# Phase 0 of a macaron layer (mixture of experts, linear attention, mixture of experts): fewer filler matmuls ahead of the first up, the first downs between the first ups, and single tiles normalised and transposed behind the ups

## The chip, the cores and the metric

One core of one Trainium2 chip runs the whole program. The metric is device time in microseconds, the median of several executions. The engines are PE (TensorE), DVE (VectorE), ACT (ScalarE), POOL (GpSimd) and SP (SyncE, which here only issues DMAs). They run in parallel, each through its own list of instructions in order, and wait for each other on semaphores.

## What is computed

x is 2 x 2048 x 128, float32. Every expert of the feed-forward blocks maps 128 to 512 and back to 128.

```python
x = x + 0.5 * ffn(layernorm(x))      # 4 experts, each row goes to the argmax of its gate
x = x + attn(layernorm(x))           # linear attention, features elu(.) + 1 of 32 projections
x = x + 0.5 * ffn(layernorm(x))      # the same weights again

def ffn(x):
    idx = argmax(softmax(x @ Wg + bg))
    h = gelu(x @ W1[e] + b1[e])      # for each expert e
    y = h @ W2[e] + b2[e]
    return y of expert idx
def attn(x):
    q, k, v = x @ Wq.T, x @ Wk.T, x @ Wv.T
    q_, k_ = elu(q @ proj) + 1, elu(k @ proj) + 1
    return q_ @ (k_.T @ v) / sum(q_)     # per batch
```

## The kernel before

The two batches pass through the two feed-forward blocks one after the other, so there are four phases, ph = 0 to 3: block 0 of batch 0, block 0 of batch 1, block 1 of batch 0, block 1 of batch 1. The attention of a batch lies beside the phases that follow.

**Tiles and visits.** The 2048 rows of a batch are sorted by expert. DVE and PE work out for each place of the sorted order which row stands there (route_hot, route_slots, route_hots, inverse, route_src), POOL gathers the rows by indirect DMA, one DMA per tile of 128 rows (L433, T = 16 tiles), and the phase computes V = 19 visits, a visit being a tile with one expert; where a tile holds rows of two experts it is visited twice, and a mask chooses the rows. s = ph * 19 + v numbers the visits.

**One visit** goes through these helpers:
- norm (DVE, L699) subtracts the mean of a gathered tile and multiplies by its deviation's inverse, into one of 8 buffers xn. It waits for the gather.
- turn_in (PE, L954) transposes one or two such tiles (a "group", by the table GROUPS) into the one PSUM bank TR, and copy_in (ACT, L1138) copies them to hT_in.
- copy_slab (SP, L342) copies the visit's first weights, with bias, to one of 7 buffers slab; the first few copies also wait for a norm, slab(s) for the norm of tile s-1 (L351).
- up (PE, L963) multiplies, 4 matmuls written as 8 instructions, into one of 3 PSUM banks U; it waits for copy_in of its tile (need, L959), for its slab and for the gelu three visits back.
- gelu (ACT, L1144) is 4 instructions from U to one of 5 buffers hT.
- down (PE, L974) multiplies by W2 into one of 2 banks DN; it waits for its gelu and for the finish two visits back.
- residual (L711) adds the second bias to the rows, finish (L723) the result of down; both on DVE.

**The order is written out by hand.** Every engine has its own loop over s. On PE, step s of the loop does down(s), then the groups due at this step (GROUP_AT, L210, by groups_of), then up(s+3) (UP_LEAD = 3). On ACT it does the copy_in of the due groups, then gelu(s+3). On DVE it does finish(s), then the norms due (NORM_LATE for phase 0, L213, by norms_of), then residual(s+2), then statistics and routing. In phase 0 tiles 0 to 3 are turned in before the loop, tile 4 at step 0, tile 5 at step 1, and after that two tiles at a time at steps 2, 4, 6, 8 and 10; the norms of tiles 5 to 15 stand at steps 0, 1, 1, 2, 3, 4, 5, 6, 6, 8 and 9. In step s POOL waits for finish(s-1) (begun, L449) and issues the gather of tile s+8; between two gathers it clears a scratch tile (rested, L419), and in steps 3 and 4 a power (pow_front, L399) takes the place of that.

**Beside phase 0** lie the routing of batch 1 (hot_at = HOT0 = 5: route_hot on DVE at the end of step 5, L615 to L623; counts on PE in step 7, L927; route_slots on DVE at the end of step 6, L628 to L640, which waits for counts; route_hots in step 7, L645; inverse on PE in step 9, L937; route_src on DVE in step 9; the visit tables at the end of step 10, L652 to L676) and the attention's side work of batch 0 (side_turn on PE at L988 and side_kq at L995, the TURNS at v = 9, 12 and 15 and one in the next phase; la_scaled on DVE at L744, steps 10, 13 and 16). la_sum (PE, L1006) belongs to the first steps of phase 1.

**Ahead of phase 0**, busy(n) (L895) issues n filler matmuls of 128 x 128 float32, two instructions each, whose results nobody reads. 24 calls stand before tile 0 is turned in, and 3 between turn_in and up of each of tiles 0, 1 and 2. DVE does norm(0) to norm(4), with the statistics and variance of batch 1 (front_stats, front_variance, L544 to L555) between them.

Of the kernel before, what the change touches and what calls it, by code (L numbers as in the profile page):

```python
# [34 lines left out]
def build(nc, x, wq, wk, wv, proj, w1, b1, w2, b2, wg, bg, out):  # L35
# [5 lines left out]
    NE, _, F = w1.shape  # L41
    R = proj.shape[1]
    NC = F // P
    T = L // P
# [22 lines left out]
    with ExitStack() as ctx:  # L67
# [141 lines left out]
        GROUPS = ((0, 1), (1, 1), (2, 1), (3, 1), (4, 1), (5, 1), (6, 2), (8, 2), (10, 2), (12, 2), (14, 2))  # L209
        GROUP_AT = (-4, -3, -2, -1, 0, 1, 2, 4, 6, 8, 10)  # L210


        NORM_LATE = (-5, -4, -3, -2, -1, 0, 1, 1, 2, 3, 4, 5, 6, 6, 8, 9)  # L213
        NORM_MID = (-6, -5, -4, -3, -2, -1, 0, 0, 2, 2, 3, 3, 5, 5, 6, 6)
# [1 line left out]

        def groups_of(ph, v):

            return ([(ph, j) for j, at in enumerate(GROUP_AT) if at == v] +
                    [(ph + 1, j) for j, at in enumerate(GROUP_AT) if at + V == v and ph + 1 < 2 * B])  # L220

        def group(ph, j):
            return ph * len(GROUPS) + j

        def group_of_tile(k):
            ph, t = divmod(k, T)
            return group(ph, max(j for j, (first, _) in enumerate(GROUPS) if first <= t))

        def norms_of(ph, v):
            def at(p):  # L230
                return (NORM_LATE, NORM_MID, NORM_EARLY, NORM_LATE)[p]
            return ([(ph, t) for t in range(T) if at(ph)[t] == v and (ph, v) != (0, 0)] +
                    [(ph + 1, t) for t in range(T) if ph + 1 < 2 * B and at(ph + 1)[t] + V == v])

        def tau(ph, t):
# [128 lines left out]
        def _(eng):  # L364
# [113 lines left out]
            for v in range(V):  # L478
                s = v
                begun(s)  # L480
                if v in (3, 4):
                    pow_front(1, v - 3)
                if v + EARLY0 < T:
                    gather(0, 0, v + EARLY0, second=v in (3, 4))
                if v == HOT0 + 2:
                    place_tiles(1)
                if v >= FIRST0:
                    gather(0, 1, v - FIRST0)
                attention_pow(0, v)
            for v in range(V):  # L490
                s = V + v
# [11 lines left out]
            for v in range(V):  # L503
                s = 2 * V + v
# [18 lines left out]
        def _(eng):  # L523
# [293 lines left out]
            front_stats(1, H, H + GS)  # L817
            norm(0, 1)
            front_stats(1, H + GS, T)
            norm(0, 2)  # L820
            front_variance(1, 1)
            norm(0, 3)
            load_rows(0, 0)
            for s in range(RES_LEAD):
# [2 lines left out]
            for s in range(2 * B * V):  # L827
                ph, v = divmod(s, V)
                f, b = divmod(ph, 2)
                o = ph - 1  # L830
                if ph in (1, 2) and v == 3:
                    la_kv(o)
                finish(s)
                if ph in (1, 2):
                    if v == 1:
                        la_features(o, 2, NG)
                        la_z(o, 0, NG)
                    if v == 2:
                        la_gt(o)
                    if v == 4:  # L840
                        lb_x2(o, 1)
                        lb_x2(o, 2)
                    if v == 5:
                        lb_x2(o, 3)
                r = (0, 1) if ph == 0 else (1, ph - 1)
                hot_at = HOT0 if ph == 0 else HOT1
                if ph in (1, 2) and v == hot_at + 2:
                    route_hots(ph + 1)
                if ph < B + 1 and v == hot_at + (3 if ph == 2 else 4):
                    route_src(*r)  # L850
                if ph == 0 and v == 0:
                    norm(0, 5)
                for ahead in norms_of(ph, v):
                    norm(*ahead)
                if ph in (1, 2) and v == 0:
                    la_scaled(o, NG - 1)
                if ph == 0 and v == hot_at + 2:
                    route_hots(1)
                if s + RES_LEAD < 2 * B * V and not full(s + RES_LEAD):
                    residual(s + RES_LEAD)  # L860
                if (ahead := chunk_ahead(s, RES_LEAD + 1)):
                    load_rows(*ahead)
                if ph == 0 and 11 <= v < 17:
                    split_b2(v - 11)
                if f == 0:
                    for t in stats_of(ph, v):
                        la_stat(b, t)
                    for g in range(NG - 1):
                        if v == VAR_AT[ph][g]:
                            la_variance(b, g)  # L870
                        if v == SCALED_AT[ph][g]:
                            la_scaled(b, g)
                if f == 0 and v == 18:
                    la_variance(b, NG - 1)
                if ph in (1, 2):
                    if v == 0:
                        la_features(o, 0, 2)
                    if v == 3:
                        lb_x2(o, 0)
                if ph < B + 1:  # L880
                    if v == hot_at:
                        route_hot(*r)
                    if v == hot_at + 1:
                        route_slots(*r)
                    if v == hot_at + 5:
                        visit_ends()
                        visit_tables(*r)
                        visit_masks(*r)
# [3 lines left out]
        def _(eng):  # L892
# [53 lines left out]
                expert_at.update({ph * V + v + i: e for i, e in enumerate(loaded(eng, v_exp, ph, v, D))})  # L946

            def turn_in(ph, j):
                first, n = GROUPS[j]
                need(eng, ffn["norm"], tau(ph, first + n - 1))  # L950
                need(eng, ffn["xTs"], group(ph, j) - 1)
                for i in range(n):
# [107 lines left out]
            front_gate(NG + 3)  # L1060
            load_visits(0, 0)
            eng.wait_ge(s_foldd, 6)
            busy(24)
            for t in range(UP_LEAD):
                turn_in(0, t)
                busy(3)
                up(t)
            turn_in(0, 3)
            eng.wait_ge(s_w["w2"], 16 * NE)
            for s in range(2 * B * V):  # L1070
                ph, v = divmod(s, V)
                hot_at = HOT0 if ph == 0 else HOT1
                o = ph - 1
                if ph in (1, 2) and v == 0:
                    side_turn(o, NG - 1)
                down(s)
                if ph in (1, 2):
                    if v == 3:
                        la_kv(o)
# [2 lines left out]
                        lb_num(o, 1)  # L1082
                    if v == 5:
                        lb_num(o, 3)
                for ahead in groups_of(ph, v):
                    turn_in(*ahead)
                if ph in (1, 2):
                    if v == 0:
                        side_kq(o, NG - 1)
# [5 lines left out]
                    inverse(ph + 1, 0, NG)  # L1095
                if s + UP_LEAD < 2 * B * V:
                    up(s + UP_LEAD)
                if (ahead := chunk_ahead(s, UP_LEAD + 1)):
                    load_visits(*ahead)
                if ph < B and v in TURNS:  # L1100
# [13 lines left out]
        def _(eng):  # L1114
# [18 lines left out]
                eng.activation(XR[0][:, lo:hi, 0:D], X0[0][:, lo:hi, :], ACT.Copy).then_inc(s_copied, 1)  # L1133

            def copy_in(ph, j):
                first, n = GROUPS[j]
                need(eng, ffn["xT"], group(ph, j))
                ffn["xTs"].done(eng.activation(hT_in[ph % 2][:, first * P:(first + n) * P], TR[:, 0:n * P], ACT.Copy))  # L1138

# [57 lines left out]
            copy_in(0, 0)  # L1197
            copy_in(0, 1)
            gelu(0)
            copy_in(0, 2)  # L1200
            gelu(1)
            copy_in(0, 3)
            gelu(2)
            for s in range(2 * B * V):
                ph, v = divmod(s, V)
                if ph in (1, 2) and v == 0:
                    side_copy((ph - 1) * NG + NG - 1)
                for ahead in groups_of(ph, v):
                    copy_in(*ahead)
                late = ph in (1, 2) and v in (0, 1, 2)  # L1210
                if ph in (1, 2):
                    o = ph - 1
# [8 lines left out]
                        la_q(o)  # L1221
                if s + UP_LEAD < 2 * B * V and not (late and v < 2):
                    gelu(s + UP_LEAD)
                if ph < B and v in TURNS:
                    side_copy(ph * NG + TURNS.index(v))
                hot_at = HOT0 if ph == 0 else HOT1
# [32 lines left out]
```

## Time and profile before

| | us |
|---|---|
| median of 3 executions | 232.36 |
| lowest and highest | 231.41, 233.33 |
| the profiled execution | 232.38 |
| its span, first to last instruction | 230.6 |

The span is what the rows below count in, from 0; 1.8 us lie around it. A row of a timeline gives the start in us, the duration in us, then engine, line, operation, what is written and read, the shape, and how many instructions of this kind follow each other (x8); in brackets how long the engine sat idle before it and what ended that. Consecutive instructions overlap, so the duration of one can reach past the start of the next. Busy over the span: PE 205.0 us (89%), DVE 158.2 (69%), POOL 158.9 (69%), ACT 129.0 (56%). The granted TensorE clock is 0.977 in the mean; it is full except near the end of the kernel.

### The profile page before, as it was taken

The numbers are of one execution on the slowest core, as the hardware profiler recorded it, in microseconds if no ns is written. First come the engines' busy times: TensorE is split into PE (matmuls) and PEld (weight loads), VectorE is DVE, ScalarE is ACT, GpSimd is POOL, SyncE is SP. The second block draws the span as 40 slices with busy tenths as digits, with TensorE's granted clock in tenths as the row PEclk, the third lists the DMA queues.
The fourth block names the chain that finished last, engine by engine and source line by source line (L and its number), as shares of the span: only waits on it lengthen the run. The fifth ranks groups of instructions, "written<-read, shape, count | busy, mean of one in ns | idle before, by whom it ended". The sixth has DMA issues, their size and how long they took to land.

```text
span 230.6 us, 6363 instructions
## 1 busy us (share of the span) xinstructions
PE 205.0 (89%) x1786; PEld 192.7 (84%) x1786; DVE 158.2 (69%) x633; ACT 129.0 (56%) x410; POOL 158.9 (69%) x222
## 2 busy tenths in 40 slices
PE   7889999985999989998999899999999999999700
PEld 7879999974899987778999797879899999999700
DVE  2799845459888979899978777899967454544300
ACT  0655057655746578436756568724776666766300
POOL 7223888971738786293274978869788888888775
PEclk9999999999999999999999999999999999999955
DMA  4998378782435553357405653435926867561111
GB/s 100 320 372 284 105 250 297 263 296 73 174 115 181 171 182 97 130 187 284 165 13 199 216 192 98 140 111 196 340 90 228 278 214 236 220 218 48 46 57 46
DMA packets 22502, 41.69 MB, mean 181 GB/s; under 512 B 3635, under 2 KB 8643, under 8 KB 22470
## 3 DMA queue, kind: packets, MB, share of 16 engines
q1 hardware_dynamic: 18496, 34.24, 40.5%
q0 software_dynamic: 3072, 6.82, 11.3%
q8 instruction: 16, 0.26, 0.4%
q10 hardware_dynamic: 902, 0.23, 0.4%
q14 instruction: 16, 0.13, 0.2%
HBM read 9.41 MB, written 6.82 MB: 70 GB/s over the span
## 4 chain that ended last, share of the span: by engine, by line
PE 27%; POOL 17%; DVE 13%; issue 11%; DMA 7%; DVEq 1%; POOLq 0%
PE U L963 11%; PE DN L974 11%; DMA G<-rows,src 7%; POOL out_dram L445 6%; POOL rest L419 4%; POOL G L433 3%; POOL RS L404 2%; DVE ST L790 2%; DVE SL L645 2%; POOL G L409 2%; DVE G L723 1%; DVE G L787 1%; PE TR L954 1%; PE S L1006 1%; PE S L1030 1%
## 5 line engine op out<-in xcount | busy, mean ns | idle before, releaser
L1144 ACT ACTIVATE hT<-U,slab 128x128 f32<-128x128 f32 x304 | 86.4, 370 | 50.1 <-PE U L963 49.2
L974 PE MATMUL DN<-W,hT 128*128 (+1 forms) x608 | 81.5, 277 | 1.7 <-DVE G L723 1.4
L963 PE MATMUL U<-hT_in,slab 128*128 (+1 forms) x608 | 81.8, 278 | 0.3
L974 PEld LDWEIGHTS DN<-W,hT 128*128 128x128 f32 x608 | 73.8, 192 | 2.8 <-issue 2.7
L963 PEld LDWEIGHTS U<-hT_in,slab 128*128 128x128 f32 x608 | 73.9, 192 | 1.8 <-issue 1.1
L433 POOL DMA_INDIRECT G<-rows,src x64 | 62.6, 978 | 13.9 <-issue 9.9
L723 DVE SCALAR_TENSOR_TENSOR G<-DN,mask,G 128x128 f32 (+1 forms) x76 | 26.4, 347 | 28.9 <-PE DN L974 25.8
L419 POOL MEMSET rest<- 128x512 f32 (+1 forms) x75 | 34.3, 457 | 8.5 <-DVE G L723 3.4
L445 POOL DMA_INDIRECT out_dram<-G x32 | 31.5, 983 | 9.0 <-issue 6.5
L699 DVE TENSOR_SCALAR xn<-G 128x128 f32<-128x128 f32 x64 | 22.3, 377 | 7.0 <-DMA G<-rows,src 6.9
L1138 ACT ACTIVATE hT_in<-TR 128x128 f32<-128x128 f32 (+1 forms) x44 | 14.5, 330 | 19.2 <-PE TR L954 18.8
L711 DVE SCALAR_TENSOR_TENSOR G<-slab,mask,G 128x128 f32 (+1 forms) x60 | 21.0, 350 | 6.0 <-DVE G L723 4.5
L404 POOL TENSOR_TENSOR RS<-VE,neghalf 128x4 f32<-128x4 f32 x8 | 8.3, 1040 | 12.6 <-DVE VE L735 12.5
L895 PE MATMUL DN<-mean_w 128*128 128x128 f32 x104 | 14.4, 297 | 1.3 <-POOL mean_w L365 1.1
L954 PE MATMUL TR<-ident,xn 128*128 128x128 f32 x64 | 14.4, 277 | 0.8 <-DVE xn L699 0.8
L895 PEld LDWEIGHTS DN<-mean_w 128*128 128x128 f32 x104 | 13.6, 210 | 1.4 <-POOL mean_w L365 1.1
L465 POOL TENSOR_TENSOR AV<-A,lane_f 128x256 bf16<-128x256 bf16 x4 | 3.3, 834 | 14.9 <-DVE A L640 14.9
L409 POOL TENSOR_TENSOR G<-VE,neghalf 128x4 f32<-128x4 f32 x8 | 8.3, 1054 | 5.0 <-DVE VE L793 4.9
L399 POOL TENSOR_TENSOR XR<-VE,neghalf 128x8 f32<-128x8 f32 x4 | 6.7, 1676 | 5.1 <-DVE VE L555 5.1
L728 DVE BATCH_NORM_STATS2 ST<-G 128x6 f32<-128x128 f32 x32 | 8.7, 286 | 1.8 <-issue 1.5
L954 PEld LDWEIGHTS TR<-ident,xn 128*128 128x128 f32 x64 | 8.4, 145 | 1.2 <-DVE xn L699 1.2
L645 DVE TENSOR_TENSOR SL<-slot_i,lane_b 128x512 bf16<-128x512 int32 x12 | 9.2, 816 | 0.0
(163 smaller groups left out, 220.2 us busy)
## 6 DMA issues: line engine op xcount, KB each, us to landing
slab<-W SPq DMA_DIRECT2D x76, 322.0 KB, 3.1
rows<-XR SPq DMA_DIRECT2D x4, 576.0 KB, 4.8
rows<-G SPq DMA_DIRECT2D x8, 288.0 KB, 2.1
X<-in_L_attn_x_dram SPq DMA_DIRECT2D x4, 256.0 KB, 6.5
XR<-in_L_attn_x_dram SPq DMA_DIRECT2D x2, 512.0 KB, 9.3
W<-in_L_ffn_W_dram SPq DMA_DIRECT2D x1, 1024.0 KB, 11.9
W<-in_L_ffn_W_dram SPq DMA_DIRECT2D x4, 256.0 KB, 5.8
G<-rows,src POOLq DMA_INDIRECT x64, 3.1
```

Of the source, the lines that this page charges most:

```text
L419: eng.memset(rest[:, 0:columns], 0.0)
L433: eng.indirect_dma_start(out=row(f, b, t, 0, RW), out_offset=None, in_=(rows0, rows1)[f][b], in_offset=bass.IndirectOffsetOnAxis(ap=src[f] ...
L445: eng.indirect_dma_start(out=out_rows, out_offset=bass.IndirectOffsetOnAxis(ap=index, axis=0), in_=row(1, b, t), in_offset=None, engine_se ...
L699: ffn["norm"].done(eng.tensor_scalar(xn[k % NXN][:, :], row(f, b, t), row(f, b, t, D, 1), row(f, b, t, D + 1, 1), ALU.subtract, ALU.mult))
L711: ffn["res"].done(eng.scalar_tensor_tensor(out=r, in0=slab[s % NSLAB][:, F + NC:SW], scalar=mask[f][b][:, v:v + 1], in1=r, op0=ALU.mult, o ...
L723: ffn["out"].done(eng.scalar_tensor_tensor(out=r, in0=DN[s % 2][:, 0:D], scalar=mask[f][b][:, v:v + 1], in1=r, op0=ALU.mult, op1=ALU.add))
L895: eng.matmul(DN[0][:, 0:P], mean_w[:, :], mean_w[:, :], start=True, stop=True)
L954: last = eng.transpose(TR[:, i * P:(i + 1) * P], xn[k % NXN][:, :], ident[:, :])
L963: i = eng.matmul(U[s % 3][:, c * P:(c + 1) * P], slab[s % NSLAB][:, c * P:(c + 1) * P], hT_in[ph % 2][:, bass.ds(v * P - expert_at[s], P)] ...
L974: i = eng.matmul(DN[s % 2][:, 0:D], hT[s % NHT][:, c * P:(c + 1) * P], W2[:, bass.ds(expert_at[s] + c * NE * D, D)], start=(c == 0 and not ...
L1138: ffn["xTs"].done(eng.activation(hT_in[ph % 2][:, first * P:(first + n) * P], TR[:, 0:n * P], ACT.Copy))
L1144: i = eng.activation(hT[s % NHT][:, c * P:(c + 1) * P], U[s % 3][:, c * P:(c + 1) * P], ACT.Gelu, bias=slab[s % NSLAB][:, F + c:F + c + 1])
```

## The change

The tables: phase 0 gets groups of one tile each (GROUPS0), tile t at step t - 4 (GROUP_AT0), and its norms stand at the same steps (NORM_SINGLE), so the norm of tile t for t of 5 to 15 is in step t - 4. In steps 0 to 11 of phase 0 (late_turns) PE turns a tile in after up(s+3) instead of before it, and ACT copies it after gelu(s+3) instead of before it. Ahead of the loop PE does busy(10) instead of busy(24) and no fillers ahead of up(2); down(0) is done after up(1), down(1) after tile 3 is turned in; the loop's downs run one visit ahead in steps 1 to 3 (downs_of) and as before from step 5. POOL's two powers and the gathers that go with them without a clearing move from steps 3 and 4 to steps 2 and 3. On DVE the variance of the second half of batch 1 moves ahead of norm(2), and norm(5) from step 0 to step 1.

```diff
+        GROUPS0 = tuple((t, 1) for t in range(T))
+        GROUP_AT0 = tuple(t - 4 for t in range(T))
+        NORM_SINGLE = (-5, -4, -3, -2, -1) + tuple(t - 4 for t in range(5, T))
...
+        def late_turns(ph, v):
+
+            return ph == 0 and v < T - 4
+
+        def downs_of(s):
+
+            return () if s in (0, DOWNS_AHEAD) else (s + 1,) if s < DOWNS_AHEAD else (s,)
+
+        DOWNS_AHEAD = 4
...
-                if v in (3, 4):
-                    pow_front(1, v - 3)
+                if v in (2, 3):
+                    pow_front(1, v - 2)
                 if v + EARLY0 < T:
-                    gather(0, 0, v + EARLY0, second=v in (3, 4))
+                    gather(0, 0, v + EARLY0, second=v in (2, 3))
...
             front_stats(1, H + GS, T)
+            front_variance(1, 1)
             norm(0, 2)
-            front_variance(1, 1)
             norm(0, 3)
...
-                if ph == 0 and v == 0:
-                    norm(0, 5)
...
-            busy(24)
+            busy(10)
             for t in range(UP_LEAD):
                 turn_in(0, t)
-                busy(3)
+                if t < 2:
+                    busy(3)
                 up(t)
+                if t == 1:
+                    eng.wait_ge(s_w["w2"], 16 * NE)
+                    down(0)
             turn_in(0, 3)
-            eng.wait_ge(s_w["w2"], 16 * NE)
+            down(1)
...
-                down(s)
+                for done in downs_of(s):
+                    down(done)
...
-                for ahead in groups_of(ph, v):
-                    turn_in(*ahead)
+                if not late_turns(ph, v):
+                    for ahead in groups_of(ph, v):
+                        turn_in(*ahead)
...
                     up(s + UP_LEAD)
+                if late_turns(ph, v):
+                    for ahead in groups_of(ph, v):
+                        turn_in(*ahead)
...
             gelu(0)
+            gelu(1)
             copy_in(0, 2)
-            gelu(1)
             copy_in(0, 3)
             gelu(2)
...
-                for ahead in groups_of(ph, v):
-                    copy_in(*ahead)
+                if not late_turns(ph, v):
+                    for ahead in groups_of(ph, v):
+                        copy_in(*ahead)
...
                     gelu(s + UP_LEAD)
+                if late_turns(ph, v):
+                    for ahead in groups_of(ph, v):
+                        copy_in(*ahead)
```

## Rows read from the trace of the kernel before

**Rows 1.** The page, part 4: chain that ended last, share of the span by engine.

```profile
PE 27%; POOL 17%; DVE 13%; issue 11%; DMA 7%; DVEq 1%; POOLq 0%
```

**Rows 2.** Busy time by window: stretch, length, PE, PEld, DVE, ACT, POOL, clock, DMA.

```profile
45.00:66.50 21.50, 17.89 (x157) 16.39 (x157) 16.12 (x66) 11.97 (x39) 11.69 (x16) 1.00 0.49 173
66.50:84.00 17.50, 16.39 (x144) 15.78 (x142) 16.05 (x62) 10.82 (x37) 12.12 (x16) 1.00 0.51 178
```

**Rows 3.** Timeline of PE: fillers at the start and ahead of tile 0, up(3), up(4).

```profile
1.06 3.35 PE L895 MATMUL DN<-mean_w 128*128 128x128 f32 x14 [1.06 <-POOL mean_w L365]
...
23.33 5.60 PE L895 MATMUL DN<-mean_w 128*128 128x128 f32 x48 [0.25 <-issue]
...
35.20 1.09 PE L963 MATMUL U<-hT_in,slab 128*128 x8
...
37.13 1.06 PE L963 MATMUL U<-hT_in,slab 128*128 x8
```

**Rows 4.** Timeline of DVE: norms of tiles 0 and 2.

```profile
25.11 0.63 DVE L699 TENSOR_SCALAR xn<-G 128x128 f32<-128x128 f32 x1 [0.21 <-DMA G<-rows,src]
...
29.70 0.48 DVE L699 TENSOR_SCALAR xn<-G 128x128 f32<-128x128 f32 x1 [1.39 <-DMA G<-rows,src]
```

**Rows 5.** Timeline of SP's DMA queue: the issue of slab(3).

```profile
30.29 0.49 SPq L342 DMA_DIRECT2D slab<-W  x1
```

**Rows 6.** The page, part 6: slab copies of the whole kernel, KB, us to landing.

```profile
slab<-W SPq DMA_DIRECT2D x76, 322.0 KB, 3.1
```

**Rows 7.** DMA issues of the first 60 us: the slab copies.

```profile
slab<-W SPq DMA_DIRECT2D x18, 322.0 KB, 3.9
```

**Rows 8.** DMA issues from 15.9 to 16.5 us: the last quarter of W2.

```profile
W<-in_L_ffn_W_dram SPq DMA_DIRECT2D x1, 256.0 KB, 7.6
```

**Rows 9.** Timeline of ACT: gelu(3), then the copy of tile 5.

```profile
36.33 1.14 ACT L1144 ACTIVATE hT<-U,slab 128x128 f32<-128x128 f32 x4 [0.46 <-PE U L963]
37.34 0.29 ACT L1138 ACTIVATE hT_in<-TR 128x128 f32<-128x128 f32 x1
```

**Rows 10.** Timeline of DVE, 46 to 58 us: norms 11, 13, routing, finish(7), finish(8).

```profile
46.12 0.35 DVE L699 TENSOR_SCALAR xn<-G 128x128 f32<-128x128 f32 x1 [0.85 <-DMA G<-rows,src]
...
47.60 0.24 DVE L615 TENSOR_TENSOR lgm<-S,XR 128x64 f32<-128x64 f32 x1
...
52.00 0.35 DVE L699 TENSOR_SCALAR xn<-G 128x128 f32<-128x128 f32 x1 [2.03 <-DMA G<-rows,src]
...
52.77 0.27 DVE L628 TENSOR_TENSOR_SCAN cum<-S,zeros 128x64 f32<-128x64 f32 x1
...
54.79 0.34 DVE L723 SCALAR_TENSOR_TENSOR G<-DN,mask,G 128x128 f32 x1
...
58.33 0.35 DVE L723 SCALAR_TENSOR_TENSOR G<-DN,mask,G 128x128 f32 x1
```

**Rows 11.** Timeline of PE: counts, up(12), up(13), up(15).

```profile
49.52 0.20 PE L927 MATMUL S<-hot,ones_b 128*128 128x64 bf16 x1 [0.65 <-DVE hot L623]
...
57.85 1.15 PE L963 MATMUL U<-hT_in,slab 128*128 x8
...
60.89 1.15 PE L963 MATMUL U<-hT_in,slab 128*128 x8
...
65.45 1.06 PE L963 MATMUL U<-hT_in,slab 128*128 x8
```

**Rows 12.** Timeline of DVE: la_scaled of the first side turn, finish(11).

```profile
62.95 0.17 DVE L744 COPY LGX<-S 128x16 f32<-128x16 f32 x1 [0.34 <-PE S L995]
...
66.56 0.35 DVE L723 SCALAR_TENSOR_TENSOR G<-DN,mask,G 128x128 f32 x1
```

**Rows 13.** Timeline of PE: two side turns and la_sum, with their waits.

```profile
73.92 0.66 PE L988 MATMUL S<-ident,G 128*128 128x128 f32 x4 [0.24 <-DVE G L723]
...
81.92 0.66 PE L988 MATMUL S<-ident,G 128*128 128x128 f32 x4 [0.77 <-DVE G L723]
...
87.66 0.99 PE L1006 MATMUL S<-G,KR 128*32 128x128 f32 x16 [0.40 <-DVE KR L756]
```

More of the change, by code:

```diff
@@ L217, in groups_of, with groups @@
         def groups_of(ph, v):
-            return ([(ph, j) for j, at in enumerate(GROUP_AT) if at == v] +
+            return ([(ph, j) for j, at in enumerate(GROUP_AT if ph else GROUP_AT0) if at == v] +
                     [(ph + 1, j) for j, at in enumerate(GROUP_AT) if at + V == v and ph + 1 < 2 * B])
+        def groups(ph):
+            return GROUPS if ph else GROUPS0
         def group(ph, j):
-            return ph * len(GROUPS) + j
+            return sum(len(groups(p)) for p in range(ph)) + j
         def group_of_tile(k):
             ph, t = divmod(k, T)
-            return group(ph, max(j for j, (first, _) in enumerate(GROUPS) if first <= t))
+            return group(ph, max(j for j, (first, _) in enumerate(groups(ph)) if first <= t))
+        def late_turns(ph, v):
[3 more added lines that the diff above has]
+        DOWNS_AHEAD = 4
         def norms_of(ph, v):
             def at(p):
-                return (NORM_LATE, NORM_MID, NORM_EARLY, NORM_LATE)[p]
-            return ([(ph, t) for t in range(T) if at(ph)[t] == v and (ph, v) != (0, 0)] +
+                return (NORM_SINGLE, NORM_MID, NORM_EARLY, NORM_LATE)[p]
+            return ([(ph, t) for t in range(T) if at(ph)[t] == v] +
                     [(ph + 1, t) for t in range(T) if ph + 1 < 2 * B and at(ph + 1)[t] + V == v])
@@ L948, in turn_in @@
             def turn_in(ph, j):
-                first, n = GROUPS[j]
+                first, n = groups(ph)[j]
                 need(eng, ffn["norm"], tau(ph, first + n - 1))
@@ L1135, in copy_in @@
             def copy_in(ph, j):
-                first, n = GROUPS[j]
+                first, n = groups(ph)[j]
                 need(eng, ffn["xT"], group(ph, j))
```

## The prediction

> **What bounds the kernel now.** I read the chain that ended last first: it is spread over PE (27%), POOL (17%) and DVE (13%), with 11% that nothing shown explains, so no engine is "the" bound and the stretch has to be followed instruction by instruction [rows 1]. The windows show where slack is. From 45 to 66.5 us PE has 17.89 of 21.5 us and DVE 16.12; from 66.5 to 84 us DVE has 16.05 of 17.5 us, about as full as its semaphores let it be [rows 2]. So after 66.5 us the end is set by when DVE gets going on visit 11, not by PE.
>
> The start of phase 0: PE runs 48 filler instructions from 23.33 us for 5.60 us although tile 0 is normalised at 25.11 + 0.63 us; the first up cannot come before those and the next 6, at 29.6, and up(3) comes at 35.20 [rows 3, 4]. From there a step (down, transposition, up) costs 1.93 us, up(3) to up(4), about 0.9 each for up and down and 0.1 for a transposition [rows 3]. Between 45 and 60 us DVE is what is late: it waits 0.85 and 2.03 us for gathered tiles 11 and 13, and behind it come the routing of batch 1 (route_hot, route_slots, route_hots) and finish(7) and finish(8) [rows 10].
>
> **The change part by part.** Half a microsecond either way decides here, so I follow each engine's order. Times are of this profiled execution.
>
> *Fillers.* 14 calls of busy go ahead of tile 0 and 3 ahead of up(2); a call is two instructions, so 34 instructions (the announced 28 are those of the first group). One is 5.60/48 = 0.117 us [rows 3]. The 20 that stay end at 23.33 + 2.33 = 25.7, when xn(0) is ready (25.74). Transposition, 6 fillers, up(0) at 26.6. up(1) needs xn(1) (27.5 us; fillers again) and comes at 28.4. down(0) needs gelu(0) and W2; W2's last quarter lands 7.6 us after an issue at 15.9, at 23.5 us, so that wait costs nothing [rows 8]. down(0) is at 29.3, rather than one us ahead of up(3) at 34.2.
>
> *Variance and norms.* front_variance(1,1), seven instructions on 8 columns each, goes into the 1.39 us that DVE waits for tile 2 before 29.70 [rows 4]; whatever of it does not fit makes norm(2) late, half a microsecond at most by this gap. It clears the way for norm(3), which then waits for its own gather, one behind tile 2's in POOL's queue. What hangs on norm(3) is slab(4), and up(4) has 2.45 us more than up(3). So I take nothing, between 0.5 later and nothing.
>
> *What starts up(3).* slab(3) is issued once norm(2) is done, at 30.29 us, and nothing in the change makes that earlier; a slab takes 3.1 us in the median of the kernel, so up(3) starts at 33.4 [rows 5, 6]. Copies and gelu(2) would let it go at 32.8. Gain here 1.8 us (35.20 to 33.4). With 3.9 us, the median of the first 60 us [rows 7], it would be 34.2; that is the late end.
>
> *The new wait.* This is the item that decides. ACT now does copy_in(s+4) after gelu(s+3), and up(s+4) needs that copy. So the ups form a loop of their own: an up ends 1.09 us after it starts and the gelu starts 0.04 later (up(3) 35.20, gelu 36.33), 1.01 to the next ACT instruction (36.33 to 37.34), the copy 0.29, and about 0.06 for the release: 2.45 us a step, against 1.93 [rows 3, 9]. Queued behind the copy on ACT is the next gelu, behind the up on PE the next transposition and down. PE waits 0.5 us in each of steps 0 to 11, unless something later is slower anyway. up(8) is at 33.4 + 5 x 2.45 = 45.7 us and up(9) at 48.1, when the old kernel at 1.93 a step has up(8) at 44.9. The head start is used up before the routing begins. I take 2.45; its bounds are 1.93 (the copy gets through unseen) and 2.6.
>
> *Gathers and powers.* POOL issues what it did, with the two powers a step earlier, so tile 10 comes one power later and tile 11 at about its old time. DVE waited for tiles 11 and 13 at steps 5 and 6 and had them at 46.12 and 52.00; norm(11) is now asked for at step 7 and norm(13) at step 9, some 53 and 59 us. Both waits, 0.85 + 2.03 us, go, and POOL has 7 us to spare there [rows 10].
>
> *Routing, with the norm behind it.* Now PE's transposition of tile s+4 waits in step s for a norm behind finish(s).
> - Step 5: down(5) ends at 45.3; finish takes some 0.3, norm, residual, register loads and stats 1.48 (46.12 to 47.60), and route_hot, 1.9 up to counts, which waited for it (its 49.52 is the first of rows 11), runs from 47.0 to 48.9 [rows 10, 11]. finish(6), norm(10), transposition 49.5, down(7), counts: route_slots at 50.75, not 52.77 (2.0 earlier).
> - Step 7: slots take 2.02 (52.77 to 54.79), finish(7) 52.8, norm(11) done 53.35, down(8), up(11) 54.4. The three route_hots, residual, stats and variance take 3.3 (58.33 - 54.79 less finish's 0.3): finish(8) 56.65 against 58.33, norm(12) done 57.2 [rows 10].
> - Step 9: transposition 12 and down(9) end at 58.2 and only then comes the inverse, 0.6: up(12) at 58.8 against 57.85. up(13) follows the loop at 61.25, then transposition 14 and side_kq at 62.3, and la_scaled 1.07 later (it waits for side_kq) at 63.35, not 62.95 [rows 11, 12]. The 1.7 us that DVE was early are lost to this order.
> - Step 10: la_scaled and the visit tables hold DVE for 3.61 us (62.95 to 66.56) [rows 12]. finish(11) at 66.95 instead of 66.56, and then norm(15), 0.3, which used to be done two steps earlier. PE, with up(14) through at 65, waits 2.5 us for it: transposition 15 at 67.55, up(15) at 68.6 against 65.45 [rows 11]. A new stall, PE 3.1 us late.
>
> *What of the 3.1 us stays.* DVE is full until 84 us and only 0.4 + 0.3 = 0.7 us late. PE's order replayed from up(15) at 68.6 to the side turn that stood at 81.92: 7 ups and 6 downs of 0.9, 2 side turns of 0.5, 2 side_kq of 0.9 and 4 transpositions of 0.1, 14.9 us, so 83.5, which is 1.6 late, since the old order held waits for DVE, 0.24 at 73.92 and 0.77 at 81.92 the longest [rows 13]. From there to la_sum at 87.66 PE has 5.2 us of work against 5.74: 88.7, 1.05 late; and of the 0.99 us that la_sum's 16 matmuls took I take 0.4 as waiting for the second half of KR, which now goes. 0.65 us stay, about DVE's own lateness, which is what has to come out where both are tied. From there on PE is full and nothing of phases 1 to 3 is changed, so the shift stays. This is my weakest term: between 0.3 and all of the 3.1.
>
> Sum, as lateness against before: up(3) -1.8; the loop and the routing bring +2.75, so up(12) is at +0.95; up(13) is at +0.35, for the old kernel lost 0.6 there; the stall brings +2.8, so up(15) is at +3.15; PE's slack takes 2.5 of that back. 0.6 us later. The profiled execution took 232.38 us (span 230.6 and 1.8 around it), the median is 232.36, so no correction: **233.0 us**, no measurable change. About 1% (2.3 us) is what a measurement of this kernel can tell from none.
>
> *The clock.* The granted clock is 1.00 in both windows, also where PE is without work for 3.6 of 21.5 us [rows 2], and I count nothing. At the lower level (1.2 GHz) the first 14 fillers took 3.35 us, 0.24 each, twice the 0.117 at 2.4 GHz [rows 3].
> The Trainium skill, TensorE: Matmul & The Clock Gate (§ HAM oscillation), says that waits between short groups of matmuls can send the array back to the slow clock each time; the new kernel adds such waits in a dozen steps. By the row the sum stays 0.6, by that rule it is the fourth case below.
>
> **The rivals.**
> 1. *The copy is not what ends last (faster).* If steps 0 to 5 run at 1.93, up(8) is at 33.4 + 9.65 = 43.05, 2.6 us earlier than I put it, route_hot follows, and DVE's full stretch moves up with it, less the la_scaled order: finish(11) some 2.5 us ahead of my figure. 233.0 - 2.5 = 230.5, and with the slots no longer waiting for the counts (0.6) 229.9. For it: ACT is busy for only 11.97 of 21.5 us [rows 2]. Against it: each link is an explicit wait, and rows 9 show each duration.
> 2. *The stall stays (slower).* Place: transposition 15 in step 11, queued on PE ahead of down(12) and behind norm(15), behind 3.6 us of la_scaled and tables. It decides from the point where PE makes up less than 0.8 of the 3.1 us, that is if the waits at 73.92 and 81.92 come from something that moves along with PE (side turns wait for finishes, which wait for downs). All of it kept is 3.1 us: 235.5. For it: PE is 16.39 of 17.5 us full there, and the waits that I can name make 1.4 us, not 2.5 [rows 2, 13]. Against it: DVE is not emptier.
> 3. *The head start is kept (the change does what it says).* Then the shift of 2.9 us at up(0) would reach the end: 229.5. It would need both the loop and the slab order not to bind; I count it with rival 1.
> 4. *The clock falls.* The matmuls of 5 to 7 us of PE work would take twice their time: about +6, 238.4.
>
> **How the numbers follow.** Forecast case 0.58 (its own range 231.6 to 234.4: slab at 3.9 adds 0.8, a loop of 2.6 adds 0.15 for each of 6 steps, a loop of 2.3 takes as much). Rivals 1 and 3 together 0.18, rival 2 0.20, clock 0.04. The range 230.2 to 235.6 holds the forecast case, nearly all of rival 2 and half of rivals 1 and 3; about 0.15 stay out. Faster by over 1% (under 230.0) 0.17, with the early half of rivals 1 and 3 and a tail; slower by over 1% (over 234.7) 0.23, most of rival 2 and the clock; within 1% 0.60.
>
> **What would show it.** Right: down(0) near 29.3; up(3) at 33.4; ups 2.4 to 2.5 us apart from up(3) to up(8), with each up's wait ended by hT_in's copy on ACT; no DVE wait for gathers after tile 7; route_slots near 50.8; transposition 15 waiting over 2 us for xn; la_sum at about 88.2. Wrong: ups 1.9 apart, or a PE that is still 2 us or more late at 88 us, or a granted clock under 1 before 200 us.

## The result and the profile after

| | before | changed |
|---|---|---|
| median, us | 232.66 | 237.89 |
| lowest and highest | 231.41, 233.33 | 236.45, 238.68 |
| profiled execution (span) | 232.38 (230.6) | 238.58 (236.8) |

The ratio is 1.022, 95% interval 1.015 to 1.030: slower by some 5 us; whether by 2% the interval leaves open. Ratios here and below leave out executions more than 1.5% above the fastest of their kernel. The forecast was 233.0, no measurable change, with a range to 235.6; the measured time lies above it. Line numbers of the changed kernel differ: up is L978, down L989, turn_in L969, norm L716, finish L740, gelu L1168, copy_in L1162, la_sum L1021.

The start came as forecast. The timeline of PE in the changed kernel: up(0), down(0), up(2), down(1), up(3) to up(8), with one of the transpositions between.

```profile
26.80 1.06 PE L978 MATMUL U<-hT_in,slab 128*128 128x128 f32 x8
...
29.66 1.13 PE L989 MATMUL DN<-W,hT 128*128 x8
...
31.60 1.15 PE L978 MATMUL U<-hT_in,slab 128*128 x8 [0.70 <-ACT hT_in L1162]
...
32.70 1.06 PE L989 MATMUL DN<-W,hT 128*128 x8
33.59 1.06 PE L978 MATMUL U<-hT_in,slab 128*128 x8
...
36.77 1.15 PE L978 MATMUL U<-hT_in,slab 128*128 x8 [0.85 <-ACT hT_in L1162]
...
39.51 1.15 PE L978 MATMUL U<-hT_in,slab 128*128 x8 [0.58 <-ACT hT_in L1162]
...
42.25 1.15 PE L978 MATMUL U<-hT_in,slab 128*128 x8 [0.58 <-ACT hT_in L1162]
43.24 0.27 PE L969 MATMUL TR<-ident,xn 128*128 128x128 f32 x1
44.98 2.07 PE L978 MATMUL U<-hT_in,slab 128*128 x8 [1.47 <-ACT hT_in L1162]
...
48.63 1.15 PE L978 MATMUL U<-hT_in,slab 128*128 x8
```

up(3) is at 33.59 (forecast 33.4, before 35.20 [rows 3]). Then up(4) to up(7) wait for hT_in, as foreseen, but 2.74 us apart and not 2.45. up(7) takes 2.07 us where the others take 1.1: after a wait of 1.47 us the matmuls run at half the clock. This wait is longer than the 0.58 of the steps around it because step 4 of the new order has no down. The busy time by window shows two stretches at the lower clock with the one between them (columns as in rows 2), and the whole from 26 to 70 us:

```profile
44.90:48.60 3.70, 3.62 (x17) 3.56 (x17) 0.00 (x0) 1.31 (x5) 2.89 (x4) 0.54 0.81 286
48.60:58.40 9.80, 7.31 (x55) 6.31 (x54) 7.87 (x29) 4.51 (x17) 3.58 (x5) 1.00 0.45 154
58.40:65.60 7.20, 6.39 (x44) 5.75 (x44) 4.48 (x20) 3.10 (x10) 2.15 (x3) 0.53 0.24 92
...
26.00:70.00 44.00, 36.36 (x264) 33.04 (x265) 23.63 (x93) 21.50 (x78) 28.80 (x35) 0.88 0.53 184
```

The granted clock was 0.54 and 0.53 there, which is the lower level (1.2 GHz) nearly throughout, and 1.00 between them; before it was 1.00 from 45 to 84 us [rows 2]. Ahead of the first stretch PE had waited 1.47 us, in the second's run-up 1.92. These are PE's rows of the second stretch and of the stall for tile 15, then la_sum:

```profile
57.27 0.33 PE L969 MATMUL TR<-ident,xn 128*128 128x128 f32 x1 [1.92 <-DVE xn L716]
...
58.46 1.80 PE L978 MATMUL U<-hT_in,slab 128*128 x8
60.67 0.47 PE L969 MATMUL TR<-ident,xn 128*128 128x128 f32 x1 [0.41 <-DVE xn L716]
61.54 2.07 PE L989 MATMUL DN<-W,hT 128*128 x8 [0.39 <-ACT hT L1168]
...
63.88 1.86 PE L978 MATMUL U<-hT_in,slab 128*128 x8
...
73.39 0.33 PE L969 MATMUL TR<-ident,xn 128*128 128x128 f32 x1 [2.13 <-DVE xn L716]
...
74.67 1.06 PE L978 MATMUL U<-hT_in,slab 128*128 x8
...
95.14 0.65 PE L1021 MATMUL S<-G,KR 128*32 128x128 f32 x16
```

up(12) is at 63.88 (57.85 before [rows 11]), up(15) at 74.67 (65.45), la_sum at 95.14 (87.66 [rows 13]). la_sum no longer waits for KR (0.65 us for 16 matmuls, 0.99 before): PE is late now, not DVE. The timeline of DVE gives the same steps: route_slots at 54.30 (52.77 before [rows 10]), la_scaled at 69.48 (62.95 [rows 12]), finish(11) and norm(15) at 72.73 and 73.00.

```profile
54.30 0.29 DVE L645 TENSOR_TENSOR_SCAN cum<-S,zeros 128x64 f32<-128x64 f32 x1 [1.34 <-PE S L943]
...
69.48 0.17 DVE L761 COPY LGX<-S 128x16 f32<-128x16 f32 x1 [1.09 <-PE S L1010]
...
72.73 0.35 DVE L740 SCALAR_TENSOR_TENSOR G<-DN,mask,G 128x128 f32 x1
73.00 0.34 DVE L716 TENSOR_SCALAR xn<-G 128x128 f32<-128x128 f32 x1
```

### The profile page after: what moved, and what is told of

The parts are those of the page before. It is cut to its first block, busy times and chain, and to the rows that moved or that the text cites. A ratio compares the mean times of both kernels' runs of the same rounds, so it can differ in the third digit from the quotient of the medians.

```text
span 236.8 us, 6304 instructions
## 1 busy us (share of the span) xinstructions
PE 206.2 (87%) x1752; PEld 193.1 (82%) x1752; DVE 159.6 (67%) x633; ACT 128.8 (54%) x415; POOL 158.9 (67%) x222
## 4 chain that ended last, share of the span: by engine, by line
PE 35%; POOL 14%; DVE 11%; issue 8%; DMA 5%; ACT 1%; DVEq 1%; POOLq 0%
PE U L978 15%; PE DN L989 14%; POOL out_dram L462 6%; DMA G<-rows,src 5%; POOL rest L436 4%; POOL G L450 2%; POOL G L426 2%; PE S L1010 2%; DVE ST L807 1%; DVE G L740 1%; PE TR L969 1%; POOL RS L421 1%; DVE SL L662 1%; DVE G L804 1%; ACT hT L1168 1%
## 5 line engine op out<-in xcount | busy, mean ns | idle before, releaser
L1168 ACT ACTIVATE hT<-U,slab 128x128 f32<-128x128 f32 x304 | 86.4, 370 | 61.5 <-PE U L978 60.6
L978 PE MATMUL U<-hT_in,slab 128*128 (+1 forms) x608 | 84.5, 283 | 4.8 <-ACT hT_in L1162 4.5
L989 PE MATMUL DN<-W,hT 128*128 (+1 forms) x608 | 83.5, 282 | 0.5 <-ACT hT L1168 0.4
L978 PEld LDWEIGHTS U<-hT_in,slab 128*128 128x128 f32 x608 | 76.0, 197 | 7.2 <-issue 6.8
L989 PEld LDWEIGHTS DN<-W,hT 128*128 128x128 f32 x608 | 75.3, 195 | 2.1 <-issue 1.6
L740 DVE SCALAR_TENSOR_TENSOR G<-DN,mask,G 128x128 f32 (+1 forms) x76 | 26.5, 348 | 36.7 <-PE DN L989 33.1
L716 DVE TENSOR_SCALAR xn<-G 128x128 f32<-128x128 f32 x64 | 23.9, 393 | 2.8 <-DMA G<-rows,src 2.6
L1162 ACT ACTIVATE hT_in<-TR 128x128 f32<-128x128 f32 (+1 forms) x49 | 15.6, 318 | 18.2 <-PE TR L969 17.8
L969 PE MATMUL TR<-ident,xn 128*128 128x128 f32 x64 | 15.8, 284 | 4.8 <-DVE xn L716 4.7
L969 PEld LDWEIGHTS TR<-ident,xn 128*128 128x128 f32 x64 | 8.8, 147 | 6.1 <-DVE xn L716 6.0
L910 PE MATMUL DN<-mean_w 128*128 128x128 f32 x70 | 10.3, 305 | 1.3 <-POOL mean_w L382 1.1
L910 PEld LDWEIGHTS DN<-mean_w 128*128 128x128 f32 x70 | 9.8, 220 | 1.5 <-POOL mean_w L382 1.1
L1045 PE MATMUL S<-KV,QT 128*128 128x512 f32 x16 | 8.8, 630 | 0.4 <-DVE G L804 0.4
```

What stands on the lines that cost most here:

```text
L716: ffn["norm"].done(eng.tensor_scalar(xn[k % NXN][:, :], row(f, b, t), row(f, b, t, D, 1), row(f, b, t, D + 1, 1), ALU.subtract, ALU.mult))
L740: ffn["out"].done(eng.scalar_tensor_tensor(out=r, in0=DN[s % 2][:, 0:D], scalar=mask[f][b][:, v:v + 1], in1=r, op0=ALU.mult, op1=ALU.add))
L910: eng.matmul(DN[0][:, 0:P], mean_w[:, :], mean_w[:, :], start=True, stop=True)
L969: last = eng.transpose(TR[:, i * P:(i + 1) * P], xn[k % NXN][:, :], ident[:, :])
L978: i = eng.matmul(U[s % 3][:, c * P:(c + 1) * P], slab[s % NSLAB][:, c * P:(c + 1) * P], hT_in[ph % 2][:, bass.ds(v * P - expert_at[s], P)] ...
L989: i = eng.matmul(DN[s % 2][:, 0:D], hT[s % NHT][:, c * P:(c + 1) * P], W2[:, bass.ds(expert_at[s] + c * NE * D, D)], start=(c == 0 and not ...
```

## The experiments

**A marker.** All differences between these kernels lie in phase 0, ahead of la_sum. In some profiled executions, of kernels that are the same up to there, tile 0 comes 1 to 3 us later than in others; in the five that are 1.3 us or more late the clock had fallen before 25 us. So I count from the start of norm(0) to the start of la_sum, in one profile of each kernel. Before: 87.66 - 25.11 = 62.55 us. Changed: 95.14 - 25.21 = 69.93 us. Two profiles of one kernel (b2 and c2) differ by 1.4 us in it, so less than that is read only where the ratio says the same, or where the ups between show in which steps it arises.

| kernel | marker, us | ratio to before | interval |
|---|---|---|---|
| before | 62.55 | 1 | |
| changed | 69.93 | 1.022 | 1.015 to 1.030 |
| a1: changed, waits filled | 68.29 | 1.019 | 1.014 to 1.025 |
| a2: changed, copy ahead of gelu | 64.14 | 1.006 | 1.002 to 1.010 |
| a3: before, fewer fillers | 61.39 | 0.990 | 0.986 to 0.994 |
| b1: changed, norms 14, 15 early | 65.59 | 1.014 | 0.997 to 1.031 |
| b2: copy ahead, norms 10 to 15 early | 60.26 | 0.986 | 0.973 to 0.998 |
| b3: a3 and early downs | 61.25 | 0.998 | 0.992 to 1.003 |
| b4: changed, 24 calls ahead of tile 0 | 72.01 | 1.026 | 1.012 to 1.040 |
| c1: changed, norms 10 to 15 early | 64.47 | 1.005 | 1.001 to 1.008 |
| c2: b2 again | 58.88 | 0.990 | 0.985 to 0.995 |
| c3: changed, slabs at once | 68.21 | 1.020 | 1.013 to 1.027 |
| c4: b2, slabs at once | 59.69 | 0.989 | 0.984 to 0.993 |

a1 to a3 ran in one session in which every kernel, also the one before (247.6 us), took some 15 us more; in the three profiles that lies after 165 us, in phase 3, where PE waited for norms and DVE up to 7.6 us for something that the profile does not name. Their ratios are read, not their times, and they hold only if this loss is the same in each kernel of that session; the markers end before it. In the other sessions the kernel before took 233.29 (b1 to b4) and 232.18 us (c1 to c4).

**a1, the waits filled.** It asks what the fall of the clock costs by itself.

```diff
+                if 1 <= s <= 12:
+                    fill(s + UP_LEAD, 6 if s == 4 else 3)
                 if s + UP_LEAD < 2 * B * V:
                     up(s + UP_LEAD)
+                if s in (7, 8, 11):
+                    fill(s + UP_LEAD + 1, 6)
```

fill(s, n) issues n filler calls into the bank that up(s) will overwrite.

> The changed kernel with filler matmuls put into the places where TensorE waits in phase 0: 3 calls (6 instructions, 0.70 us) ahead of each of up(4) to up(15), 6 ahead of up(7), and 6 (1.4 us) ahead of the transpositions of tiles 11, 12 and 15. Nothing else changes. Theory A (the clock): the changed kernel is slow partly because the granted clock fell from about 45 to 48.3 and from 58.5 to 65.3 us after TensorE had waited 1.47 and 1.92 us; with the waits filled the clock stays 1.00 over 40 to 70 us and the kernel is 2 to 3 us faster than the changed one: 235 to 236. Rival B (the waits themselves are all of it, the lower clock is hidden behind VectorE): clock 1.00, time unchanged at 237.9 or longer by the fillers that outlast their waits, up to 2 us.

The window from 26 to 70 us, to be set beside the same line of the changed kernel above:

```profile
26.00:70.00 44.00, 42.99 (x375) 41.03 (x375) 25.49 (x106) 22.01 (x80) 28.63 (x35) 1.00 0.53 185
```

The clock holds at 1.00. The marker shortens by 1.6 us, of the 7.4 that are lost. That alone is hardly more than two profiles of one kernel differ, and the ratio, 1.019, does not tell the two kernels apart. It is also too small a price, since some fillers outlast their wait; b1 and c3 below give 2.4. So the clock is part of the loss, the smaller part.

**a2, the copy ahead of the gelu.** On ACT, the copies of phase 0 stand ahead of the step's gelu, as before the change; PE's order stays.

```diff
-                if not late_turns(ph, v):
-                    for ahead in groups_of(ph, v):
-                        copy_in(*ahead)
+                for ahead in groups_of(ph, v):
+                    copy_in(*ahead)
...
-                if late_turns(ph, v):
-                    for ahead in groups_of(ph, v):
-                        copy_in(*ahead)
```

> The changed kernel with one part undone: ScalarE copies the tile of a step ahead of the step's gelu again, TensorE's order stays. Theory A (the loop up, gelu, copy, up makes the steps 2.74 us long, and its idle time is what lets the clock fall): ups come 1.9 to 2.0 us apart from up(4) to up(8), the clock holds, and the kernel comes to 231 to 233.5, near the kernel before. Rival B (the norm behind finish and the late tile 15 make the loss): ups are 1.9 apart but route_slots, tile 12 and tile 15 still stall TensorE, the clock may fall after one of these stalls, 235 to 237.

The marker is 5.8 us shorter, and its profile has no fall of the clock between 26 and 70 us. The loop is open: PE's timeline of a2, up(3) to up(8).

```profile
34.93 1.06 PE L978 MATMUL U<-hT_in,slab 128*128 x8
...
37.21 1.15 PE L978 MATMUL U<-hT_in,slab 128*128 x8
...
39.59 1.15 PE L978 MATMUL U<-hT_in,slab 128*128 x8 [0.23 <-ACT hT_in L1162]
...
41.62 1.06 PE L978 MATMUL U<-hT_in,slab 128*128 x8
...
43.34 1.15 PE L978 MATMUL U<-hT_in,slab 128*128 x8 [0.55 <-issue]
...
45.48 1.06 PE L978 MATMUL U<-hT_in,slab 128*128 x8
```

10.55 us for five steps, 2.1 each, where the changed kernel took 15.04. PE still waited 1.4, 2.3, 1.2 and 2.4 us ahead of the transpositions of tiles 10, 11, 12 and 15, for their norms (of the first the profile says only "issue"): both theories hold in part, and 1.6 us over the kernel before are left.

**a3, the fillers alone.** The kernel before with busy(10) for busy(24) and no fillers ahead of up(2).

> The kernel before with the 17 filler calls (34 instructions, 4.0 us) taken out as in the change, nothing else: the order of downs, tiles and copies stays. Theory A (the head start is lost in what comes after in any case, since slab(3) and slab(4) come after norms and the gathers come at POOL's pace): 231.5 to 233, no difference that can be told. Rival B (the fillers are dead weight on the path): up(3) 2 to 3 us earlier and the end 2 to 3 us earlier, 229.5 to 230.5. Rival C (the fillers hold the clock up): the clock falls below 1.00 before 60 us and the kernel is 2 us or more slower.

1.2 us less by the marker, ratio 0.990: between A and B. The head start of up(0) is 2.6 us; what becomes of it is in PE's timeline of a3:

```profile
26.90 1.06 PE L963 MATMUL U<-hT_in,slab 128*128 128x128 f32 x8
...
30.84 1.15 PE L963 MATMUL U<-hT_in,slab 128*128 x8 [0.83 <-DMA slab<-W]
...
33.88 0.33 PE L954 MATMUL TR<-ident,xn 128*128 128x128 f32 x1 [0.88 <-ACT hT L1145]
34.17 1.15 PE L963 MATMUL U<-hT_in,slab 128*128 x8
```

up(2) waits for slab(2), up(3) is only 1.0 us earlier than before [rows 3]; later DVE waits 2.12 us for tile 11. No fall of the clock there, so rival C is out: the fillers were not what held the clock in phase 0.

**b1, norms 14 and 15 one step earlier.**

```diff
-        NORM_SINGLE = (-5, -4, -3, -2, -1) + tuple(t - 4 for t in range(5, T))
+        NORM_SINGLE = (-5, -4, -3, -2, -1, 1, 2, 3, 4, 5, 6, 7, 8, 9, 9, 10)
```

> The changed kernel with norm(14) and norm(15) each one step earlier on VectorE (14 in step 9, 15 in step 10, so 15 stands ahead of la_scaled and the visit tables), nothing else. In the changed kernel TensorE stood 2.13 us before transposition 15 for them. Theory A (VectorE is the bound there, the stall is hidden by its full stretch up to 90 us): transposition 15 waits less than 0.5 us, up(15) 2 us or more earlier, but la_sum moves by less than 0.7 us and the total stays within 0.5% of the changed kernel. Rival B (the stall is paid): la_sum and the end 1.5 to 2.2 us earlier than in the changed kernel.

PE's timeline of b1 around transposition 15, which used to wait 2.13 us:

```profile
69.26 0.27 PE L969 MATMUL TR<-ident,xn 128*128 128x128 f32 x1
69.37 1.06 PE L989 MATMUL DN<-W,hT 128*128 x8
71.01 1.15 PE L978 MATMUL U<-hT_in,slab 128*128 x8 [0.58 <-ACT hT_in L1162]
```

The wait is gone and the marker 4.3 us shorter. b1's profile has one stretch of 3.4 us at the lower clock in this part where the changed kernel's had 10. Cut at the ups, the markers tell the two causes apart:

| us | norm(0) to up(8) | up(8) to up(12) | up(12) to up(15) | up(15) to la_sum | lower clock |
|---|---|---|---|---|---|
| changed | 23.42 | 15.25 | 10.79 | 20.47 | 3.4 and 6.8 us, in the first two parts |
| a1 | 22.25 | 14.73 | 10.85 | 20.46 | none |
| b1 | 22.51 | 13.80 | 8.25 | 21.03 | 3.4 us, in the second |
| c1 | 23.30 | 11.71 | 8.26 | 21.20 | 3.4 us, in the first |
| c3 | 22.47 | 13.80 | 11.48 | 20.46 | 3.4 us, in the third |

Up to up(12) b1's code is that of the changed kernel, and it comes 2.4 us earlier there; c3, with no fall up to there, does so too (and b1's own fall shows no price against c3). That is the price of the changed kernel's two falls (0.9 and 1.5). a1 loses 0.9 of it again in the second part, where its fillers outlast waits. The other 2.0 us of b1's 4.3 arise behind up(12): they are the norms' (2.5 at the stall, 0.6 lost again behind it). So rival B holds in size, and what falls is A, my step that DVE's full stretch hides this stall.

**c1, norms 10 to 15 one step earlier**, with the copy still behind the gelu; tiles 10 to 15 at steps 5, 6, 7, 8, 9, 10.

> The changed kernel with the norms of tiles 10 to 15 one step earlier (the table of b2), but with ScalarE's copy behind the gelu as in the change. Counted from the start of norm(0) to la_sum, the kernel before took 62.55 us, the changed one 69.93, with the copy ahead (a2) 64.14, with copy and norms (b2) 60.26. Theory A (two separate costs that add up: the copy 5.8, the norms 3.9): 69.93 - 3.9, so 66 us, total ratio to the kernel before 1.010 to 1.018. Rival B (with the loop at 2.74 us a step VectorE has time and the norm's place hardly matters): 68.5 to 70. Rival C (the stalls behind the norms are what lets the clock fall, so that moving them mends the clock too): under 65.5.

64.47: 5.5 us shorter, under the bound of rival C, with one fall of the clock left. By the table above the second fall (1.5 us) went with the stalls; without it some 3.9 are left, the norms' price in theory A. That moving them mended the clock, as C has it, is not shown: c3 lacks the second fall too, with its norms where they were.

**b2 and c2, both.** The edits of a2 and c1 in one kernel.

> ScalarE's copy ahead of the gelu again (as in a2) and in addition the norms of tiles 10 to 15 one step earlier on VectorE, so that none of them stands behind route_slots or the visit tables when TensorE wants its tile. In a2 TensorE still waited 1.4, 2.3, 1.2 and 2.4 us for tiles 10, 11, 12 and 15, and its la_sum came 1.8 us after that of the kernel before once a 1.3 us later start is taken off. Theory A (what a2 still lost is the norm behind finish): these waits fall under 0.7 us each and la_sum comes at 86.5 to 88, level with or ahead of the kernel before (87.66), total ratio 0.99 to 1.00. Rival B (what is lost is VectorE's own work, whose order doesn't matter): la_sum stays at 89 to 90.

> The same kernel as b2 (copy ahead of the gelu, norms 10 to 15 one step earlier), in more rounds, to see if it beats the kernel before. The marker from norm(0) to la_sum was 2.3 us shorter than before, fillers included: if that carries to the end, the ratio is 0.985 to 0.993 and its interval excludes 1. If the shift is lost in later phases, 0.996 to 1.004.

60.26 and 58.88 us, 2.3 and 3.7 under the kernel before. PE's timeline of b2 has one wait over 0.6 us left between 48 and 66 us, and one fall of the clock (up(12) takes 2.07):

```profile
52.41 0.33 PE L969 MATMUL TR<-ident,xn 128*128 128x128 f32 x1 [1.05 <-DVE xn L716]
53.00 1.15 PE L989 MATMUL DN<-W,hT 128*128 x8 [0.26 <-issue]
...
54.54 2.07 PE L978 MATMUL U<-hT_in,slab 128*128 x8
```

The repeat had no fall at all in this part: from up(12) to up(13) it took 2.77 us where b2 took 4.07, which is nearly all of the 1.4 us between their markers. It took 229.46 us against 232.18, ratio 0.990 with 1 outside its interval: this version beats both kernels, the one before by 1%, as c2's expectation had it; b2 came out a little beyond its theory A.

**b3, the early downs.** a3 with down(0) after up(1), down(1) after tile 3 and downs_of in the loop.

> The kernel before with 34 filler instructions fewer (a3) and the downs of the change: down(0) after up(1), down(1) after tile 3, downs one visit ahead in steps 1 to 3; groups, norms, transpositions and copies as before. a3 alone had la_sum 1.0 us earlier and a ratio of 0.990. Theory A (early downs only fill waits): la_sum within 0.5 us of a3's 86.7, ratio 0.985 to 0.995. Rival B (early downs lengthen the wait for up(3), or let the clock fall): la_sum 1 us or more later than a3's.

Marker 61.25 against a3's 61.39: they are worth nothing by themselves. (By the clock of the run la_sum is at 89.44, but norm(0) at 28.19.) The ratio, 0.998, is over that of a3, and its interval overlaps a3's only at the edge; part of it may be a late start, which its profiled execution had.

**b4, the fillers back in the changed kernel**, busy(24) ahead of tile 0.

> The changed kernel with only the 14 calls ahead of tile 0 back (24 calls, 3.3 us more), nothing else. Theory A (the loop sets the pace, and the falls of the clock come from waits inside it): start 3.3 us later, of which 1.5 to 3 remain at la_sum (96.5 to 98), the granted clock still falls between 45 and 70 us; total 0 to 2 us over the changed kernel. Rival B (removing these fillers is why the clock falls): clock 1.00 over 40 to 70 us, la_sum under 95.

Marker 72.01, 2.1 us over the changed kernel (this profiled execution was 4 us over its median of 239.02). The clock still falls twice between 50 and 72 us. Theory A, at the lower end of its figures. The 3 calls ahead of up(2) were not put back: they write into the bank that down(0) now fills before them, and no run has all 17 back.

**c3 and c4, the slabs at once**, in the changed kernel and in b2.

```diff
-                if s > 1:
-                    need(eng, ffn["norm"], s - 1)
                 copy_slab(s)
```

> The changed kernel with slab(2) to slab(4) issued as soon as the visit table is there, without waiting for norms 1 to 3. In the changed kernel up(4) started at 36.77 us, 0.8 us after its tile was copied, and slab(4) was issued at 31.88. Theory A (up(3) and up(4) wait for slabs that hang on the norms): up(3) comes 0.5 to 0.8 us after norm(0) + 7.6 instead of + 8.4, up(4) 2.5 to 2.8 us after up(3) instead of 3.2, the marker from norm(0) to la_sum 0.5 to 1.5 us shorter than 69.93. Rival B (the slabs then get in the way of the gathers, which share the DMA engines): norms 2 to 6 wait longer for their gathers, the marker is the same or longer.

> b2 with slab(2) to slab(4) issued at once, as in c3. Theory A: up(4) 0.5 to 1 us earlier than in b2, marker 59.3 to 60.3 us, ratio up to 0.003 under that of b2. Rival B (gathers pushed back, norm(5) and norm(6) already wait 0.75 and 0.50 us for theirs in b2): marker 60.3 to 61.5 us, ratio over that of b2.

c3: up(4) follows up(3) by 2.73 us (36.90, 39.63) and not 3.18, so slab(4) was what up(4) waited for. But norm(3) now waits 1.71 us for its gather (0.94 in the changed kernel), and up(3) comes 8.8 us after norm(0) instead of 8.4. up(4) is where it was, 11.53 us after norm(0) against 11.56. The marker, 68.21, is 1.7 shorter, but with one fall of the clock instead of two, so that is the clock's; the ratio, 1.020, is the same within its interval. c4 is level with b2. What the slabs gain the gathers lose.

## Why the prediction was wrong

By the marker the change is two parts with opposite signs: fewer fillers and early downs bring 1.3 us (b3), the new order of norms, transpositions and copies costs 8.7 (61.25 to 69.93). With it go the moved powers, gathers and variance, which no run undid by themselves; b2 and c2 have them too and are faster than b3.

**Right:** the start (up(0) 26.8 for 26.6, down(0) 29.7 for 29.3, up(3) 33.6 for 33.4); that slabs and gathers eat the head start (in a3 up(2) waits for its slab and DVE 2.12 us for tile 11; c3); the closed loop up, gelu, copy, up (a2); that the waits for gathers of tiles 11 and 13 go; that norm(15) behind the visit tables stalls PE by over 2 us (2.13 for 2.5). The time of up(3) is right partly by luck: it follows down(1) without a wait, and ahead of them up(2) had waited 0.70 us, so that slab(3) set it, as I had it, is not shown.

**Wrong, by step, as lateness at the places of the sum:**
- *"2.45 us a step".* 2.74. The terms as I wrote them add up to 2.49, not 2.45. Two links were too short: an up that starts after a wait takes 1.15 us, and its gelu starts 1.19 after it (39.51 to 40.70), not 1.13; and from the end of the copy to the next up are 0.24 us, not 0.06. ACT's timeline of the changed kernel shows both, the up that follows this copy being at 42.25:

```profile
40.70 1.14 ACT L1168 ACTIVATE hT<-U,slab 128x128 f32<-128x128 f32 x4 [1.43 <-PE U L978]
41.72 0.29 ACT L1162 ACTIVATE hT_in<-TR 128x128 f32<-128x128 f32 x1
```

 The 0.06 had no row; I had taken it from a wait of another pair of engines (DVE to PE). Over the four steps to up(8) 1.2 us.
- *up(4) a step after up(3).* 3.18 us, slab(4) being late: 0.7 us. I had seen that it hangs on norm(3) and allowed it half a microsecond at most, and put nothing into the sum.
- *"The clock. ... I count nothing".* It fell twice. up(7) to up(8) took 3.65 us instead of 2.74 (0.9), and from route_slots to up(12) 9.58 instead of 8.05 (1.5, with the half-speed up(11), down(9) and up(12) in it). Rival 4 had the mechanism with 0.04 of the chances and a price of 6 us, and that the measured time came out near its 238.4 is luck: only these 2.4 us are the clock's own. The rest is the waits. The price per matmul was right (8 matmuls of up(7) took 2.07 us for 1.15), though the row I took it from does not show it: the profile gives the first 10 us a granted clock of 1.00 in spite of fillers of 0.24 us.
- *"PE's slack takes 2.5 of that back".* PE was 9.2 us late at up(15) (74.67 against 65.45) and 7.5 at la_sum, so 1.7 came back. I had let the replay end at DVE's lateness; with the loop and the clock as they were PE was 9 us late, past anything DVE could hide. In the window from 80 to 90 us PE is busy all through:

```profile
80.00:90.00 10.00, 10.00 (x92) 10.00 (x91) 9.39 (x34) 6.24 (x23) 7.07 (x10) 1.00 0.47 162
```

These and small ones (0.2 at up(3), 0.6 from up(8) to route_slots, 0.7 from up(12) to finish(11), 0.3 from there to up(15)) make up the 6.8 us between the forecast of la_sum, 88.3, and 95.14.

**The rule that I weighed**, TensorE: Matmul & The Clock Gate in the Trainium skill (§ HAM oscillation), that waits between short groups of matmuls can bring the slow clock back, was borne out in so far as it did come back. The granted clocks were 0.54 and 0.53, after waits of 1.47 and 1.92 us. My argument against it was a row of the kernel before, in which PE had gaps too and kept the clock. It was true of that row and no argument for the new kernel. But it did not come each time: a2 waited 2.27 and 2.37 us and kept the clock, c3 had the same wait of 1.47 us as the changed kernel and kept it there, b2 fell after one of 1.05 and its repeat kept it after 1.29. All five profiles with the late copy and no fillers in the waits (changed, b1, b4, c1, c3) have one or two falls between 40 and 72 us, the three with the old order (before, a3, b3) none. Which wait brings a fall stays open.

**Costs that are not independent.** The copy is worth 5.8 us alone (a2) and 4.2 with the norms early (c1 to b2); the norms 5.5 alone (c1) and 3.9 with the copy first. The falls of the clock are spread unevenly over these profiles. Taken off by the steps in which they arose (2.4 us in the changed kernel, 0.8 in c1, 1.3 in b2, none in a2), the copy is worth some 3.4 alone and 4.7 with the norms early, and the norms 3.9 and 5.2: together 8.6, more than the 7.3 of each alone. These are estimates from one profile of each kernel.

## What to carry to other kernels

Before a copy or a transposition is put behind other work, write down the cycle that closes through it, with both hand-overs between engines, and compare it with the step: here 2.74 against 1.93 us, paid in the steps from up(4) to up(10). An operand that is made one step before it is wanted needs its whole chain (finish, norm, transposition, copy) clear of the step's side work; moving six norms by one step was worth about as much as the copy. And where TensorE gets new waits, a fall of its clock belongs into the likeliest case, not into a rival of 4%.

## What the runs showed of the hardware

- From the end of an ACT copy to the first matmul that needed it 0.23 to 0.24 us passed (39.28 to 39.51, 44.74 to 44.98), where a norm on DVE was followed by its transposition after 0.05 to 0.06. Whether this is the pair of engines is not shown: up also waits for its slab and the gelu three visits back ahead of its first matmul, and takes its address from a register, which the transposition does not.
- Two stretches at the lower clock, 3.4 and 6.8 us long, cost the changed kernel 2.4 us (b1 and c3 are that much earlier at up(12)), less than the 5 us that they would cost a PE that never waits. c3 has waits of 1.40 and 1.16 us where the second of them lay.
- The clock is not the same in each execution of one kernel. The changed kernel's four executions had mean clocks of 0.955 to 0.971, and b2 fell once in one profile and not in the other. Falls before 25 us, in code that no kernel here changes, went with a tile 0 that was 1.3 to 3.1 us later in a2, b1, b3, b4 and c3.
- Three slab copies issued at once delay a gather: norm(3) waited 1.71 us for its tile in c3 and 1.69 in c4, against 0.94 to 0.98 with the slabs held back.
